# Gates of the second half made on 8 rows before their broadcast, in one core's fused block

## The reference

```
mod = (silu(c) @ wmod).reshape(8, 6, 1, 128)
sa, ca, ga, sb, cb, gb = mod[:, 0], ..., mod[:, 5]
ga = (2 * (ga >= 0) - 1) * maximum(abs(ga), 0.25)
gb = (2 * (gb >= 0) - 1) * maximum(abs(gb), 0.25)
h = layernorm(x) * (1 + ca) + sa
x = x + ga * attention_stack(h)      # 6 layers: linear attention with 8 heads, and an MLP
h = layernorm(x) * (1 + cb) + sb
x = x + gb * fp4_ffn(h)              # gated FFN on inputs and weights rounded blockwise to FP4
```

## Time and profile before

| | |
|---|---|
| Median of 3 runs | 1198.16 us (1198.06 to 1198.7) |
| Span of the profiled execution | 1196.8 us |
| PE busy | 1129.7 us (94%) |
| POOL busy | 1090.7 us (91%) |
| DVE busy | 1074.1 us (90%) |
| ACT busy | 1035.2 us (86%) |

### The profile page before, as it was taken

How to read it: one execution, slowest core, us unless ns; L and a number is a source line. 1 busy time by engine, 2 the same in 40 slices (tenths; PEclk the granted TensorE clock), 3 DMA queues, 4 the chain that set the end, 5 groups by cost and what they waited for, 6 DMA issues and landing times.

```text
span 1196.8 us, 28581 instructions
## 1 busy us (share of the span) xinstructions
PE 1129.7 (94%) x9722; PEld 864.8 (72%) x9722; DVE 1074.1 (90%) x2885; ACT 1035.2 (86%) x1776; POOL 1090.7 (91%) x920
## 2 busy tenths in 40 slices
PE   7787999999999999999999999999999888999996
PEld 5574687787777777777778778777777755565664
DVE  7889889999999999999999999999987479999973
ACT  5687999999999999999999999999998795767753
POOL 4888999999999999999999999999999888999762
PEclk8799999999999999999999999999999999999998
DMA  8121778768778777687777776866767420110000
GB/s 308 36 71 53 214 213 217 188 209 219 179 205 217 194 216 189 193 221 177 219 212 182 224 202 190 220 194 194 214 188 217 107 61 21 44 37 36 19 19 36
DMA packets 213857, 190.13 MB, mean 159 GB/s; under 512 B 113392, under 2 KB 192080, under 8 KB 213712
## 3 DMA queue, kind: packets, MB, share of 16 engines
q1 hardware_dynamic: 213712, 188.31, 56.3%
HBM read 87.06 MB, written 76.02 MB: 136 GB/s over the span
## 4 chain that ended last, share of the span: by engine, by line
POOL 34%; PE 27%; issue 22%; DVE 10%; ACT 3%; DMA 2%; SPq 2%; DVEq 0%; POOLq 0%; ACTq 0%
POOL hidden L1787 15%; POOL rows_split L1779 6%; POOL arena L1760 4%; POOL arena L1793 3%; PE pair_mlp L576 2%; PE pair_mlp L556 2%; PE ring_pair L615 2%; PE ring_pair L616 2%; PE ring_pair L617 2%; PE pair L567 2%; PE pair L599 2%; DVE ring_pair L1371 2%; DVE arena L1508 2%; PE pair_mlp L674 1%; DVE arena L1389 1%
## 5 line engine op out<-in xcount | busy, mean ns | idle before, releaser
L1787 POOL TENSOR_TENSOR hidden<-hidden 128x2048 f16<-128x2048 f32 x92 | 376.1, 4088 | 0.0
L883 ACT ACTIVATE hidden<-ring_pair,hidden_bias 128x512 f32<-128x512 f32 x384 | 245.6, 686 | 27.9 <-PE ring_pair L617 27.5
L892 ACT ACTIVATE hidden<-hidden 128x2048 f16<-128x2048 f32 x96 | 183.4, 1911 | 17.8 <-PE mlp L633 15.6
L1100 DVE BATCH_NORM_STATS2 bn<-x_all 128x6 f32<-128x128 f32 x896 | 184.2, 278 | 3.2 <-POOL x_all L1739 1.9
L1713 POOL TENSOR_TENSOR rstd<-ve,minus_half 128x8 f32<-128x8 f32 x104 | 170.5, 1640 | 0.0
L852 ACT ACTIVATE arena<-x_all,nmr,rstd 128x128 f32<-128x128 f32 x384 | 157.9, 495 | 0.0
L615 PE MATMUL ring_pair<-arena,halves 128*128 128x512 f16 x384 | 146.1, 381 | 4.5 <-DMA arena<-rows_split 2.8
L616 PE MATMUL ring_pair<-arena,halves 128*128 128x512 f16 x384 | 146.0, 380 | 0.0
L617 PE MATMUL ring_pair<-arena,halves 128*128 128x512 f16 x384 | 145.9, 380 | 0.0
L631 PE MATMUL mlp<-halves,hidden 128*128 128x128 f16 x768 | 135.9, 219 | 1.4 <-POOL hidden L1787 1.4
L633 PE MATMUL pair_mlp<-halves,hidden 128*128 128x128 f16 x768 | 136.5, 220 | 0.0
(11 more groups left out here) (206 smaller groups left out, 3145.1 us busy)
## 6 DMA issues: line engine op xcount, KB each, us to landing
n_away<-all_blocks SPq DMA_DIRECT2D x47, 512.0 KB, 3.3
norm_raw<-n_away SPq DMA_DIRECT2D x188, 128.0 KB, 3.0
k_away<-all_blocks SPq DMA_DIRECT2D x45, 512.0 KB, 2.8
q_away<-all_blocks SPq DMA_DIRECT2D x45, 512.0 KB, 3.3
arena<-k_away SPq DMA_DIRECT2D x180, 128.0 KB, 3.6
arena<-q_away SPq DMA_DIRECT2D x180, 128.0 KB, 3.6
x_all<-in_L_attn_x SPq DMA_DIRECT2D x8, 512.0 KB, 5.4
x_in<-in_L_attn_x SPq DMA_DIRECT2D x8, 512.0 KB, 4.0
```

Of the source, the lines that this page charges most:

```text
L883: act.activation(hidden_t[:, c * W + h * HALF:c * W + (h + 1) * HALF], ring[n % 2], ACT.Prelu, bias=hidden_bias[:, b:b + 1], scale=HIDDEN_ ...
L892: act.activation(half_rows(hidden_hi, h), half_rows(hidden_t, h), ACT.Copy).then_inc(hidden_hi_ready, 1)
L1100: last = nc.vector.bn_stats(bn[:, 6 * t:6 * t + 6], src(t))
L1787: pool.tensor_tensor(half_rows(hidden_lo, h), half_rows(hidden_t, h), half_rows(hidden_hi, h), ALU.subtract).then_inc(hidden_lo_ready, 1)
```

## The change

The four vectors are first made on 8 rows only, one for each sequence, by one product whose stationary operand is one column of `cond_b` for each sequence. DVE makes the gates there, in six operations of at most 8x256, reading PSUM. A second operand, `batch_rows`, holds for each sequence an 8x128 block that is one in that sequence's row. PE's eight broadcasts then multiply it by `gate_rows`, contracting over 8 rows where `cond_b` and `wmod` were contracted over 128. The eight results and ACT's copies have the size of before. PE waits for DVE's six steps ahead of the broadcasts. `prepare_gates` is gone, and what waited for its 18 steps waits for ACT's eight copies.

```diff
-    GATE_STEPS = 18
+    GATE_STEPS = 6
+        gate_rows, gate_size, gate_sign = k_exp_t[0:B, 0:4 * D], k_exp_t[0:B, 4 * D:6 * D], k_exp_t[0:B, 6 * D:8 * D]
+        batch_rows = q_exp[0:B, :]
@@ SP, load_back(0)
-                    sp.wait_ge(mod_out_steps, GATE_STEPS)
+                    sp.wait_ge(mod_out_copied, B)
@@ PE, behind L463
+            nc.tensor.matmul(ring[1][0:B, :], cond_b.rearrange("p (b k) -> p b k", b=B)[:, :, 0], wmod_s[:, 2 * D:6 * D],
+                             start=True, stop=True).then_inc(mod_in_done, 1)
             pe.wait_ge(mod_in_copied, 2)
+            pe.wait_ge(mod_out_steps, GATE_STEPS)
             for b in range(B):
                 after(pe, mod_out_copied, b - 1)
-                nc.tensor.matmul(ring[b % 2], tile(cond_b, b), wmod_s[:, 2 * D:6 * D],
+                nc.tensor.matmul(ring[b % 2], batch_rows[:, b * P:(b + 1) * P], gate_rows,
                                  start=True, stop=True).then_inc(mod_out_done, 1)
@@ DVE, between L1091 and the wait for ln_turned
+            dve.wait_ge(const_steps, IDENTITY_STEP)
+            nc.vector.tensor_copy(batch_rows.rearrange("p (b k) -> p b k", b=B),
+                                  identity[0:B, 0:B].unsqueeze(2).to_broadcast((B, B, P))).then_inc(mod_out_steps, 1)
+            dve.wait_ge(mod_in_done, 3)
+            raw = ring[1][0:B, :].rearrange("p (k d) -> p k d", d=D)
+            gated = gate_rows.rearrange("p (k d) -> p k d", d=D)
+            size, sign = (a.rearrange("p (k d) -> p k d", d=D) for a in (gate_size, gate_sign))
+            nc.vector.tensor_scalar(size, raw[:, 0::3, :], -1.0, GATE_FLOOR, ALU.mult, ALU.max).then_inc(mod_out_steps, 1)
+            nc.vector.tensor_scalar(sign, raw[:, 0::3, :], 0.0, 2.0, ALU.is_ge, ALU.mult)
+            nc.vector.tensor_copy(gated[:, 1, :], raw[:, 1, :]).then_inc(mod_out_steps, 1)
+            nc.vector.tensor_scalar(gated[:, 2, :], raw[:, 2, :], 1.0, None, ALU.add).then_inc(mod_out_steps, 1)
+            dve.wait_ge(mod_out_steps, 2)
+            nc.vector.tensor_tensor(size, size, raw[:, 0::3, :], ALU.max).then_inc(mod_out_steps, 1)
+            dve.wait_ge(mod_out_steps, 5)
+            nc.vector.scalar_tensor_tensor(out=gated[:, 0::3, :], in0=sign, scalar=-1.0, in1=size, op0=ALU.add,
+                                           op1=ALU.mult).then_inc(mod_out_steps, 1)
             dve.wait_ge(ln_turned, 1)
@@ DVE, items(v)
-                if 27 <= v < 27 + GATE_STEPS: prepare_gates(v - 27)
@@ DVE and POOL, gate(0); DVE, x_scaled(0)
-                    wait_ge(mod_out_steps, GATE_STEPS)
+                    wait_ge(mod_out_copied, B)
```

More of the change, by code:

```diff
@@ L1270, in hidden_low @@
                                         ALU.subtract).then_inc(hidden_lo_ready, 1)
[L1272 to L1295, removed]
             def weight_bounds(n):
@@ L1453, in gate @@
                 if u == 0:
-                    dve.wait_ge(mod_out_steps, GATE_STEPS)
+                    dve.wait_ge(mod_out_copied, B)
                 dve.wait_ge(x_ready, 2 * (ITEMS - B) + u + 1)
@@ L1814, in gate @@
                 if u == 0:
-                    pool.wait_ge(mod_out_steps, GATE_STEPS)
+                    pool.wait_ge(mod_out_copied, B)
                 pool.wait_ge(x_ready, 2 * (ITEMS - B) + u + 1)
```

## The result

The change made the kernel slower: 1205.72 us (1205.01 to 1206.66, 4 runs) against 1198.11 (4 runs), a ratio of 1.0057 with a 95% interval of 1.0039 to 1.0076. A second measurement beside 33 runs of the kernel before gave 1204.79 us and 1.0042 (1.0028 to 1.0056). The forecast was 1197.7, in a range up to 1200.4. The profiled execution took 1205.01 us with a span of 1203.2 (the median of the kernel before is 1198.16, its span 1196.8).

A forecast was written before the change was run, and what follows sets the result against it. PE was taken as the floor of the items, 18.27 us each. Opening +2.0 and items -2.5 made -0.5 us: span 1196.3, run 1197.7 us, range for 8 in 10 from 1195.5 to 1200.4.

The forecast's parts named there:

- the price of the broadcasts: PE's opening: the eight 8-row broadcasts were taken to cost what the 128-row ones did, 7.44 us.
- 2.0 was forecast: Opening: PE waits for DVE's gates, starts the broadcasts 2.0 us late, and the opening ends 2.0 us later (bounds 1.3 and 2.8).
- Rival 2: Opening: the 8-row products run at half clock throughout; opening +8, total +5.5, 1203.7 us; chance 0.07.
- The gain in the items: The 20 items, 18 with a gate step: removing the steps from DVE gives back 2.5 us by the count on PE.
- the floor: Items: PE, busy throughout the quiet stretch, sets the least time per item, 18.27 us.
- The mechanism I gave: Items: DVE's gate steps hold up POOL's small L1744, 0.504 us instead of 0.21, so 5.4 us over 18 items.
- The 0.2 us of room: Items: POOL runs at 18.02 us, about 0.2 below PE's 18.27, absorbing 3.6 us over 18 items.
- the 1.8 us worked out from it: Items: POOL's hold-up of 5.4 us less its room of 3.6, the lower bound of the gain.
- rival 4: Items: POOL is the bound, so the pitch falls to 18.02 and 6.7 us return; total -4.7, 1193.5 us; chance 0.07.
- Rival 1: Opening: the clock falls in PE's new idle gap, slowing two broadcasts; opening +3.9, total +1.4, 1199.6 us; chance 0.13.
- Rival 3: Opening: DVE's 4.45 us of lateness are not absorbed by idle times; total +1.95, 1200.1 us; chance 0.06.
- which I had as 1.4: Opening: DVE's lateness, after 3.07 us of idle time, makes the operation at 41.59 start 1.4 us late, at 42.95.

The follow-up runs named there:

- the padded kernel: The changed kernel with both operands of the eight broadcasts padded with zeros from 8 to 128 rows; 1201.69 and 1201.71 us, 1.0026 and 1.0023 of the kernel before.
- by the fillers: The changed kernel, broadcasts still on 8 rows, with 20 small products filling PE's idle time before the wait for the gates; 1202.46 us, 1.0038 of the kernel before.
- deferred kernels: The kernel before with its broadcasts moved behind the first transposes: full operands and 18 steps kept, 1.0013; gates on 8 rows padded to 128, 0.9968.
- the kernel before with the PSUM operand: The kernel before with one operand of DVE's six-column operation (bounds of the weights) written to PSUM instead of SBUF; 1197.21 us, ratio 0.9988.
- the padded kernel with the operand in PSUM: The changed kernel, broadcasts padded to 128 rows, with one operand of DVE's six-column operation in PSUM instead of SBUF; 1199.16 and 1198.1 us, 1.0 and 0.9998.

## Why the prediction was wrong

**The step that failed** is the price of the broadcasts: "No row has such a product with 512 columns; I take L471's time". It gave 7.44 us; they took 12.43, 5.0 more (3.7 in the second profile), and the 1.2 GHz went on under L495 (2.69 for 1.47) and L514 (once L510), so that PE's delay grew from 1.75 at their start to 6.7 at their end and 8.9 when L503 (once L499), the last bias product, starts. 1.2 us of that came back at the fillers behind it, which the kernel before also ran in part at the low clock (until 36.6 us; its start is in the earlier trace rows). So the delay was 7.7 where 2.0 was forecast, 5.9 us more than at the broadcasts' start, all of it gathered while the clock was low. Rival 2 had this mechanism at "about +6, opening +8, total +5.5, 1203.7 us"; measured were +5.0 (the eight alone), +7.0 and +6.3 of the span; the medians differ by 7.6 and 5.0. I gave it a chance of 0.07. No row of the trace spoke against it, and a product of a shape that the trace doesn't hold should have had more. The granted clock of 0.51 over L510, with PE busy throughout, was the warning: there too PE had work and lost the clock.

**The gain in the items** was the second, smaller miss: 2.5 forecast, 1.70 measured. It was mis-sized because the 2.5 us above the floor were not all gates. From 500 to 868 us of the kernel before, the idle times of PE and its weight loads ahead of L576 and of L585 are:

```profile
DMA arena<-k_away: 1.6, 4
...
DVE small L1230: 3.6, 10
```

After the change, from 505 to 875, these are 0.7 (2 times) and 0.6 (once); the sums count PE and its weight loads, so they are no times of the path. The first belongs to items that load a layer, not to the gate steps, and it comes and goes with the phase of the transfers: the items with it took up to 18.77 after the change, 18.89 before, 19.21 in the padded kernel. The mechanism I gave, POOL's small operation held up by DVE's steps, is shown by L1744 at 0.202; that PE meets DVE's lateness directly at L1230 I had not seen. The 0.2 us of room that I gave POOL rests on one pair of starts at the end of the items, 18.02 us apart; in the quiet stretch the pairs are 18.2 to 18.5 apart. That the 1.8 us worked out from it comes near the measured 1.70 is luck.

**What was right.** PE's start at 14.10 for a forecast 14.35 (raw product 0.98 for 0.93, the steps 1.92 for 2.1); L1428 at 16.32 for 16.8; floor and direction in the items; POOL isn't the bound (rival 4: no pitch fell below 18.27). Rival 1, the gap, is refuted by the padding, which keeps the gap of 2.10 us, and in its one trace by the fillers. With the clock held in the broadcasts and the collision taken out, the kernel measures 1.0 and 0.9998 of the one before, and the forecast as summed was 0.9996. That they agree is in part luck. The opening is +2.7 and +4.2 at item 5 for the forecast 2.0, of which 1.1 is the padding's own cost, and 2.0 to 2.5 us are gained behind item 43, where no step of mine had a gain and the clock stays up that was low in the kernel before. The change's ratios lie 0.0042 to 0.0059 above these two, 5 to 7 us; in its trace the low clock makes 5.9 us of PE's delay.

**Rival 3**, DVE's 4.45 not absorbed, was half right. In the change itself PE's larger delay covers it. In the padded kernel DVE does reach the maximum over the keys without idle time, 0.65 to 0.7 us late, which I had as 1.4 against PE's 2.0. What it can cost is more than that, by a collision that no step of mine had: L1310 at 2.34 us, worth 2.0 us at item 5 between two traces with the same length of low clock. In the medians the operand makes some 3 us, of which an unknown part is the clock's.

**Open**: why of two deferred kernels one waits 2.18 and the other 0.84 us for the same transfer in item 5, and the 0.85 us that the change lost behind the 20 items. I suspect the phase of the transfers, but no run separated it. Open too is what sets the length of the low clock in the opening and whether it is low near the last items.

## What to carry to other kernels

Cutting a product's contraction from 128 rows to 8 saves nothing here and cost the clock: pad the operands with zeros to the full height where many such products stand in a row, and watch the granted clock, not the busy share. Work that is needed late shouldn't stand in a queue for which everything waits. Here neither moving it alone (1.0013) nor shrinking it in its place (1.0042, padded 1.0023) made the kernel faster; both together did (0.9968). And when a profile is compared with another, compare the stretches of low clock first: profiles of this kernel with one of 3.4 us near the last items are some 2 us longer than those without. When a stage is moved by a microsecond or two, look which short operation now begins beside a long one on the other engine.

## What the runs showed of the hardware

- Matmuls over 8, 32 and 64 rows with 512 columns, eight products in a row without a pause, went from 2.4 down to 1.2 GHz 1.6 to 3.1 us after their start (1052 to 1057 ns a matmul), in all six profiles that have them; over 128 rows, with PE waiting for ACT between them, the clock held (592 ns), in all six that have these.
- A TENSOR_SCALAR or SCALAR_TENSOR_TENSOR of DVE with all operands in SBUF that begins under a long operation of POOL ends only behind it: the 128x6 one 0.02 to 0.03 us behind (2.34 us in all), and the 128x768 one 0.41 to 0.43 behind, as L1225 in the kernel before with the PSUM operand:

```profile
42.72 2.35 POOL L1740 TENSOR_TENSOR x_all<-x_all,mod_in 128x1024 f32<-128x1024 f32 x1 [0.49 <-POOL x_all L1737]
43.17 2.32 DVE L1225 TENSOR_SCALAR bo_rows<-bo_rows 128x768 f32<-128x768 f32 x1
```

It takes 0.56 where it begins ahead of POOL's (in the first profile of the padded kernel with the operand in PSUM at 48.00 against 48.11, and POOL's then takes 2.66 in place of 2.35). With one input in PSUM the 128x6 operation takes 0.17 inside POOL's, and in the padded kernel with that operand L1246 (128x768, one input in PSUM, at 45.27) keeps its 0.94 inside POOL's L1737 (44.67 to 47.05). The transposes of DVE (128x1024, SBUF to SBUF) keep their 1.23 beside POOL too (L1223 at 46.91 in the padded kernel's second profile, POOL's L1739 at 46.72). The rule of the Trainium skill that the prediction named (GPSIMD Engine Reference, Specifications: two SBUF inputs or a two-port mode contend) agrees with the 128x6 operation, which has two SBUF inputs. The other way about, POOL's 128x8 operation took up to 0.66 us in the items with a gate step and up to 0.71 in those with a step of the FFN's weights, and its 128x2048 one 4.09 in either kernel.
- The zeros cost DVE's time too: beside POOL's two memsets of 128x1024 (0.95 us) and 128x512 (0.53) an 8x128 operation of DVE on the way to `cond_b` takes 1.23, where it takes 0.29 in the kernel before, and ends 0.07 us behind the second:

```profile
2.44 0.95 POOL L1702 MEMSET arena<- 128x1024 f32 x1
2.70 1.23 DVE L1091 TENSOR_SCALAR arena<-arena 8x128 f32<-8x128 f32 x1 [2.70 <-ACT arena L806]
...
3.33 0.53 POOL L1703 MEMSET arena<- 128x512 f32 x1
```

`cond_b` is copied at 5.64 in place of 4.54, 1.1 us later, and all of PE's opening stands behind it.
